# A recommender's interaction network: base tiles by transfers, two contraction tiles to a vector instruction, and one native matmul where three rounded ones stood

## The reference

```python
# e: [2048, 39, 16], field f of sample s is tbl_f[ids[s, f]]
x = e
outs = []
for W in (W0, W1):                       # W0: [128, 39*39], W1: [128, 128*39]
    inter = (x[:, :, None, :] * e[:, None, :, :]).reshape(B, x.shape[1] * 39, 16)
    x = einsum('bid,hi->bhd', inter, W)  # [2048, 128, 16]
    outs.append(x.sum(axis=-1))
h = concatenate(outs + [dense_ctx], axis=1)        # [2048, 272]
h = maximum(h @ W_top1 + b_top1, 0)                # 512
h = maximum(h @ W_top2 + b_top2, 0)                # 256
y = h @ W_top3                                     # [2048, 1]
```

## Time and profile before

| what | value |
|---|---|
| median of 3 runs | 967.51 us (964.41 to 972.47) |
| span of the profiled execution | 1508.4 us |
| PE, DVE, ACT, POOL busy in it | 884.9, 648.8, 600.9, 623.7 us |
| mean granted TensorE clock | 0.788 |
| gathers: number, median, mean, longest | 624, 944 ns, 999 ns, 5595 ns |
| bytes moved by transfers | 88.81 MB |

### The profile page before, as it was taken

One profiled execution on the slowest core, in us unless ns is written; L12 is line 12 of the kernel. 1 busy time (PEld: TensorE's weight loads), 2 busy tenths in 40 slices (PEclk: granted clock), 3 DMA queues, 4 the chain that ended last, 5 costly groups with the idle time before them and its releaser, 6 DMA issues.

```text
span 1508.4 us, 15925 instructions
## 1 busy us (share of the span) xinstructions
PE 884.9 (59%) x3824; PEld 686.1 (45%) x3824; DVE 648.8 (43%) x1012; ACT 600.9 (40%) x1033; POOL 623.7 (41%) x628
## 2 busy tenths in 40 slices
PE   0136393719268292763958367291863936629998
PEld 0014262508146181552846256270642724527886
DVE  2015292617155282442835156160632615427870
ACT  0013282407154171532735154160532714418772
POOL 6756437461714517154271715417054071450000
PEclk9997596759678596785977678595775967859999
DMA  4112142212122132122322122121221312203320
GB/s 130 24 39 61 38 113 52 69 45 66 26 75 61 23 98 68 38 52 51 85 59 58 27 77 71 39 67 25 78 59 18 95 27 70 67 13 101 106 78 3
DMA packets 101439, 88.81 MB, mean 59 GB/s; under 512 B 59925, under 2 KB 71325, under 8 KB 101250
## 3 DMA queue, kind: packets, MB, share of 16 engines
q1 hardware_dynamic: 81410, 83.02, 18.8%
q0 software_dynamic: 19968, 5.15, 3.9%
HBM read 21.35 MB, written 10.49 MB: 21 GB/s over the span
## 4 chain that ended last, share of the span: by engine, by line
PE 38%; another core or an unknown queue 28%; issue 20%; ACT 6%; DVE 4%; POOL 2%; DMA 1%; DVEq 0%; ACTq 0%; SPq 0%; POOLq 0%
PE mlp_ps L440 7%; PE g_ps L429 6%; PE x_ps L400 5%; PE x_ps L397 5%; PE x_ps L398 5%; PE rep_ps L386 3%; POOL e_rows L346 2%; ACT G L589 2%; PE mlp_ps L471 2%; PE mlp_ps L459 2%; DVE products L739 2%; ACT product_hi L572 2%; DVE product_lo L748 1%; PE aux_ps L368 1%
## 5 line engine op out<-in xcount | busy, mean ns | idle before, releaser
L346 POOL DMA_INDIRECT e_rows<-in_tbl_dram,ids_sb x624 | 623.5, 999 | 721.3 <-DMA ids_sb<-in_ids_dram 535.7
L748 DVE TENSOR_TENSOR product_lo<-products,product_hi 117x512 fp32r<-117x512 f32 (+1 forms) x448 | 308.1, 688 | 598.7 <-remote 369.6
L572 ACT CAST product_hi<-products 117x512 fp32r<-117x512 f32 (+1 forms) x448 | 281.4, 628 | 298.7 <-remote 131.2
L400 PE MATMUL x_ps<-product_lo,w_hi 117*128 117x512 f32 (+1 forms) x448 | 199.3, 445 | 176.0 <-issue 91.8
L397 PE MATMUL x_ps<-product_hi,w_hi 117*128 117x512 f32 (+1 forms) x448 | 254.7, 569 | 9.9 <-issue 9.9
L589 ACT COPY G<-g_ps 128x320 f32 (+1 forms) x256 | 189.4, 741 | 38.2 <-remote 24.6
L400 PEld LDWEIGHTS x_ps<-product_lo,w_hi 117*128 117x128 f32 (+1 forms) x448 | 92.5, 207 | 224.1 <-issue 104.5
L398 PE MATMUL x_ps<-product_hi,w_lo 117*128 117x512 f32 (+1 forms) x448 | 190.3, 425 | 0.0
L429 PE MATMUL g_ps<-e_diag,x1T_hi 128*128 128x320 f32 x512 | 134.7, 347 | 92.6 <-issue 58.9
L440 PE MATMUL mlp_ps<-G,w1T 128*128 (+1 forms) x624 | 186.8, 400 | 0.8 <-ACT G L589 0.8
L429 PEld LDWEIGHTS g_ps<-e_diag,x1T_hi 128*128 128x128 f32 x512 | 97.6, 206 | 126.9 <-issue 82.7
(11 more groups left out here) (42 smaller groups left out, 612.7 us busy)
## 6 DMA issues: line engine op xcount, KB each, us to landing
shifted<-cycle SPq DMA_DIRECT2D x128, 234.0 KB
left<-cycle SPq DMA_DIRECT2D x192, 78.0 KB
e_scratch<-e_parts SPq DMA_DIRECT2D x16, 640.0 KB
e_diag<-e_scratch SPq DMA_DIRECT2D x512, 20.0 KB
e_rows<-in_tbl_dram,ids_sb POOLq DMA_INDIRECT x624
shifted<-cycle SPq DMA_DIRECT2D x64, 156.0 KB
w1T<-in_L_rec_W_dram SPq DMA_DIRECT2D x1, 2496.0 KB
G<-in_L_rec_W_dram SPq DMA_DIRECT2D x1, 819.0 KB
```

Of the source, the lines that this page charges most:

```text
L346: nc.gpsimd.indirect_dma_start(out=e_rows[slot][:, f * D:(f + 1) * D], out_offset=None, in_=tables[f], in_offset=bass.IndirectOffsetOnAxis ...
L400: last = nc.tensor.matmul(x1_ps[c % 2][:, :], w0_hi[0:rows, k, :], product_lo[0:rows, (c * KT + k) % LO_RING, :], start=False, stop=(k == ...
L572: nc.scalar.copy(product_hi[0:rows, n % RING, :], products[0:rows, n % RING, :]).then_inc(hi_ready, 1)
L748: nc.vector.tensor_tensor(product_lo[0:rows, n % LO_RING, :], products[0:rows, n % RING, :], product_hi[0:rows, n % RING, :].bitcast(f32), ...
```

## The change

The kernel is written anew around the same arithmetic of the first layer.

- **One tile per batch.** All programs step over 64 chunks `g`, with no loop, and the dense network runs over 128 samples instead of 256: `layer1` has 39 native matmuls of 128 columns for each tile.
- **Base tiles.** The selection matmuls, `rep_ps`, `cycle`, `left` and `shifted` are gone. ACT copies the transposed fields twice over to `eT` (78 partitions, plain float32), and `load_bases` fills five base tiles for each half tile of 1024 columns, with 14 transfers of 39 rows of 4 KB on SP. Each of the seven contraction tiles is a product of two base tiles, both in SBUF.
- **Wide products.** `multiply`, `round_products` and `lower_parts` handle a group of two contraction tiles (1024 elements a partition), and one of one: four instructions of each where there were seven. Products have one buffer.
- **Native G.** `e_diag` and `x1T` stay plain float32, and a quarter of G is one native float32 matmul in place of three float32r ones. The second split (L581's rounding and L759) becomes one plain copy. `e_diag` and its copy in DRAM are half as large.
- **G is copied** with fields outside and the eight samples inside: ACT reads PSUM with a stride and writes runs of eight floats, where it read in order and wrote each float 2 KB from the last.
- **Gathers.** All indices are loaded at the start, and `e_rows` has three slots. `copy_e` on DVE copies a tile twice over to `e_d`, in the first chunk of the tile before it, between `lower_parts` and `multiply`.
- **At the start** ACT issues 32 transfers that assemble the weights.

```diff
+E_SLOTS = 3
...
+STARTS = ((0, 0, 0), (1, 2, 3), (6, 12, 7), (31, 23, 22))
+MIXED = (0, 13)
+BASES = STARTS + (MIXED,)
+PAIRS = ((0, 1), (0, 2), (0, 3), (0, 4), (1, 2), (1, 3), (2, 3))
+NT = len(PAIRS)
+R = 3 * F
+GROUPS = ((0, 1, 2, 0), (0, 3, 2, 2), (1, 2, 2, 4), (2, 3, 1, 6))
+NG = len(GROUPS)
...
+            def load_bases(u):
+                sp.wait_ge(eT_ready, (u // 2 + 1) * ET)
+                after(sp, product_ready, (u - 1) * 2 * NG)
+                half = eT[:, :, :].rearrange("r b d -> r (b d)")[:, u % 2 * HALF:(u % 2 + 1) * HALF]
+                for a, starts in enumerate(BASES):
+                    for n, start in enumerate(starts):
+                        sp.dma_start(bases[u % 2][n * F:(n + 1) * F, a, :],
+                                     half[start:start + F, :]).then_inc(bases_ready[u % 2], 16)
...
+            for t in range(TILES):
+                if t <= 1:
+                    pool.wait_ge(ids_loaded[t], 16)
+                after(pool, e_d_ready, t - E_SLOTS + 1)
+                for f in range(F):
+                    nc.gpsimd.indirect_dma_start(
+                        out=e_rows[t % E_SLOTS][:, f * D:(f + 1) * D], out_offset=None, in_=tables[f],
+                        in_offset=bass.IndirectOffsetOnAxis(ap=ids_sb[:, t, f:f + 1], axis=0),
+                    ).then_inc(gathered[t % E_SLOTS], 16)
...
-                for n, (x, part) in enumerate(((x1T_hi, 0), (x1T_hi, 1), (x1T_lo, 0))):
-                    last = nc.tensor.matmul(g_ps[q % 2][:, :], x[:, q, :], e_diag[c % 2][:, :, q, part, :],
-                                            start=(n == 0), stop=(n == 2))
...
+                nc.tensor.matmul(g_ps[q % 2][:, :], x1T[:, q, :], e_diag[g % 2][:, :, q, :],
+                                 start=True, stop=True).then_inc(e_diag_free if q == Q - 1 else g_in_ps, 1)
...
-                nc.scalar.copy(G[:, :, bass.ds(it % 2 * NB + c * CB + q * QB, QB)].rearrange("i f b -> i b f"),
-                               g_ps[q % 2][:, :].rearrange("i (b f) -> i b f", f=FO)).then_inc(g_ready, 1)
...
+                nc.scalar.copy(G[:, :, t % 2 * TB + c * CB + q * QB:t % 2 * TB + c * CB + (q + 1) * QB],
+                               g_ps[q % 2][:, :].rearrange("i (b f) -> i f b", f=FO)).then_inc(g_ready, 1)
...
+            def copy_e(t):
+                dve.wait_ge(gathered[t % E_SLOTS], (t // E_SLOTS + 1) * 16 * F)
+                after(dve, eT_in_ps, ET * t)
+                after(dve, e_stored, 16 * t)
+                rows = e_rows[t % E_SLOTS][:, :].rearrange("b (n f d) -> b d n f", n=1, d=D)
+                nc.vector.tensor_copy(e_d[:, :, 0:2 * F].rearrange("b d (n f) -> b d n f", f=F),
+                                      rows.to_broadcast([TB, D, 2, F])).then_inc(e_d_ready, 1)
+            def multiply(g, n):
+                a, b, count, first = GROUPS[n]
+                u = g // 2
+                cols = slice(g % 2 * COLS, (g % 2 + 1) * COLS)
+                dve.wait_ge(bases_ready[u % 2], (u // 2 + 1) * 16 * LOADS)
+                after(dve, lo_ready, (g - 1) * NG + n + 1)
+                nc.vector.tensor_tensor(products[:, first:first + count, :], bases[u % 2][:, b:b + count, cols],
+                                        bases[u % 2][:, a:a + 1, cols].to_broadcast([R, count, COLS]),
+                                        ALU.mult).then_inc(product_ready, 1)
+            def lower_parts(g, n):
+                _, _, count, first = GROUPS[n]
+                dve.wait_ge(hi_ready, g * NG + n + 1)
+                after(dve, contracted, (g - 1) * NG + n + 1)
+                nc.vector.tensor_tensor(product_lo[:, first:first + count, :], products[:, first:first + count, :],
+                                        product_hi[:, first:first + count, :].bitcast(f32), ALU.subtract).then_inc(lo_ready, 1)
...
+            copy_e(0)
+            multiply(0, 0)
+            for g in range(CHUNKS):
+                t, c = divmod(g, CPT)
+                multiply(g, 1)
+                lower_parts(g, 0)
+                multiply(g, 2)
+                lower_parts(g, 1)
+                if c == 0 and t + 1 < TILES:
+                    copy_e(t + 1)
+                multiply(g, 3)
+                lower_parts(g, 2)
+                if g + 1 < CHUNKS:
+                    multiply(g + 1, 0)
+                lower_parts(g, 3)
```

More of the change, by code:

```diff
@@ L603, in relu1 @@
-            def relu1(it, pair):
-                act.wait_ge(h1_in_ps, it * 2 + pair + 1)
-                for m in (2 * pair, 2 * pair + 1):
-                    nc.scalar.activation(h1[:, m, :], mlp_ps[:, m % 2, :], ACT.Relu, bias=bias1[:, m:m + 1]).then_inc(h1_ready, 1)
-            def relu2(it):
-                act.wait_ge(h2_in_ps, it + 1)
+                    act.wait_ge(g_in_ps, g * (Q - 1) + q + 1)
+                if c == 0 and q == 0:
+                    after(act, h1_in_ps, M1 * (t - 1))
@@ new lines, in copy_y @@
+            def copy_y(t):
+                act.wait_ge(y_in_ps, t + 1)
+                after(act, y_stored, 16 * t)
+                nc.scalar.copy(y[:, :], mlp_ps[0:1, 2, :]).then_inc(y_ready, 1)
+            act.wait_ge(zeroed, 1)
+            for row, k, j, shift, count in runs:
+                halves = 1 if shift == 0 else 2
+                act.dma_start(w0_both[row:row + count, 0:halves, k, :],
+                              w0[j:j + count, 0:halves, shift, :]).then_inc(w0_loaded, 16)
@@ L654, in _ @@
             for n in range(ET):
-                copy_eT(0, 0, n)
+                copy_eT(0, n)
+            round_products(0, 0)
             act.wait_ge(mlp_loaded, 5 * 16)
-            copy_cycle(0, 0)
-            round_product(0, 0, 0)
-            for c in range(CPI):
-                chunk(0, c, first=True)
-            for c in range(CPI):
-                chunk(1, c, second=True)
-            with act.Fori(2, ITERS - 1) as it:
-                for c in range(CPI):
-                    chunk(it, c)
@@ L697, in _ @@
+            for n in range(2):
+                nc.vector.memset(bases[n][:, len(BASES) - 1, :], 0.0).then_inc(zeroed, 1)
+            for n in range(2):
+                nc.vector.memset(e_diag[n][:, :, :, :], 0.0).then_inc(e_diag_free, 1)
+            nc.vector.memset(e_d[:, :, 2 * F], 1.0)
+            dve.wait_ge(w0_loaded, 16 * len(runs))
+            nc.vector.tensor_tensor(w0_sum, w0_sum, w0_both[:, 1, :, :], ALU.add).then_inc(w0_step, 1)
             dve.wait_ge(w0_step, 1)
-            nc.vector.tensor_tensor(w0_sum, w0_sum, w0_both[:, 1, :, :], ALU.add).then_inc(w0_step, 1)
@@ L786, in _ @@
-            split_hi(0, 0, 0)
-            split_lo(0, 0)
-            multiply(0, 0, 0)
-            for c in range(CPI):
-                chunk(0, c, first=True)
-            with dve.Fori(1, ITERS - 1) as it:
-                for c in range(CPI):
-                    chunk(it, c)
-            end = ITERS - 1
-            for c in range(CPI):
-                chunk(end, c, final=True)
-            lower_x1T(end, CPI - 1)
-            lower_dense(end)
+            dve.wait_ge(dense_loaded, 16 * 3 * GAP // D)
```

739 lines of the change are left out of this document (276 added, 463 removed).

## The result

The changed kernel takes 1069.12 us (median of 4 runs, 1059.68 to 1071.16), the kernel before 969.99 in the same comparison: 1.102 times as long, 95% interval 1.096 to 1.108. The forecast was 1022 us, slower, in a range of 905 to 1090.

What follows compares the result with a forecast made beforehand. The prediction took the kernel before to be bound by gathers that DVE holds, and the changed one more so: 101.8 us of start, 14 tiles at 57.6 and 114 of end make 1022 us, against 967.5; range 905 to 1090.

Steps and rivals of the forecast that it cites:

- The kernel before is bound by its gathers, and something lengthens them: Timed runs of the kernel before: 54.3 us per tile, 5.5 more than bare gathers, against compute of 47.0.
- A gather is held while DVE reads two operands from SBUF: POOL's gathers beside DVE: held during two-SBUF-input instructions, passing when DVE waits or reads one operand from PSUM.
- The rival that rested on it: Gathers beside DVE are not held, so the changed kernel is faster, 895 to 950 us; chance 0.27.
- the rival of a fixed cost: Gathers cost 1.39 us each whatever DVE does, so the time stays the same, 976 us; chance 0.10.
- The residue: A gather meeting a holding DVE instruction waits half of it on average: 0.30 us before, 0.53 after, 1.62 a gather.
- The walk: Other count for a chunk: DVE pairs each ahead of an even 0.84 us wait, two gathers a pair, 1.43 us each.
- The door between adjacent instructions: Assumed that a gather slips in at any boundary of two DVE instructions, which the gather at 217.54 did not.
- the starved rival: Gathers never slip in between adjacent DVE instructions, one passes per wait: 74.5 us a tile, 1259 us; chance 0.10.
- PE's part: Compute on PE falls from 11.75 to 11.4 us a chunk, 45.7 a tile, and isn't the bound.
- the cover of SP's work: SP's queue: 18.9 us of issue in 22.8 for two chunks, hidden by PE's compute at no cost.
- The sum: Whole kernel: 101.8 us to start, 14 tiles of 57.6, 114 at the end, together 1022 us.
- the prediction's view from above: Difference to 967.5 us: gathers' lengthening costs 46, the later place of their waiter 19, the shorter drain gives 14.

Runs made afterwards that it cites:

- before_sb: The kernel before, with the three products a chunk that read `rep_ps` from PSUM reading the cycle tile in SBUF instead; 1012.05 us (1.050).
- the two cadence runs: No computation, only stretches of 39 gathers beside a loop of one kind of instruction, then beside seven DVE widths; 1.252 us a gather beside nothing.
- after_512: The changed kernel with each 1024-wide DVE instruction written as two of 512, also called the 512-wide kernel; 959.89 us (0.994).
- after_13: The changed kernel, but from the fourth tile on with 13 gathers a tile for 39; 953.32 us (0.988).
- the cured kernel: The changed kernel with DVE's products and lower parts both reading their second operand from a constant in PSUM; 957.14 us (0.989).

## Why the prediction was right, and where its sizes were off

*The kernel before is bound by its gathers, and something lengthens them.* Shown: without two thirds of them it takes 896 us. Its compute is 49.5 us a tile, not the 47.0 of the undisturbed stretch, so the gathers add less to compute than I thought, 4.8 us a tile for 7.3.

*A gather is held while DVE reads two operands from SBUF.* Shown from both sides: PSUM operands in after bring back 112 us, the SBUF operand in before costs 46, and by itself the hold gives 2.26 for 1.25 us. The sentence of the Trainium skill (SBUF — State Buffer, Who interferes with whom) on two SBUF inputs agrees with this; its other one, that tensor_tensor was not seen to stall a DMA, does not: here it made the gather, an indirect DMA, take 1.96 us for 0.94. The rival that rested on it, 890 to 950, fell. So did the rival of a fixed cost.

*The residue.* This was the weak step. "Half an instruction, on average" is wrong, because gather and instruction fall into step with each other. The walk's even waits of 0.84 us are not there either: in after DVE runs without a pause from 408.3 to 420.4 us, and then waits 0.98, 2.46 and 2.52 us at a time for `product_hi`. For 1024 columns the rule gave 1.62 us and the walk through a chunk 1.43; I took 1.55 between them, measured are 1.61. With 49.3 us of compute, 1.55 would give 58.3 us a tile, 1.61 gives 59.8: this term is 1.5 us of the 2.2 by which a tile was forecast too short, compute the other 0.7. For 512 columns the same rule was far off (1.45 expected, 1.31 measured, from 110 to 800 us), and for before_sb it missed the other way (22 us forecast, 46 measured). So its agreement with 54.3 us for before was partly luck, and so was how near 1.55 came to 1.61: it was taken between two countings, and neither describes how gathers and waits meet in after.

*The door between adjacent instructions,* on which the starved rival hung: it is there, and in after no gather missed it. But it is not sure. Two gathers of 624 in the two cadence runs were held to the end of the loop, and in before_sb 34 of 220 held gathers missed one or more. The gather at 217.54 was such a one. The starved rival was wrong for after, but what it rested on is real.

*PE's part.* Each record was right. The chain of waits of the 512-wide kernel (start, us, what) has the two of G in 0.54 us for 0.55, and eight of layer1 in 0.89, 0.111 each for 0.115:

```profile
500.15 0.54 PE g_ps L291 x2
...
504.38 0.89 PE z_ps L299 x8
```

Two of the last chunks start 11.07 and 10.87 us after the ones before, for 11.4. Yet a tile takes 51.3 us for 45.7. Named wrong was the cover of SP's work, "PE's 11.4 us a chunk hide it": the mean load on the queue fits, but one `spread` a tile stands behind 14 transfers, and PE then pays the wait of some 3 us and the lower clock after it. The rest of the 5.6 us I can't put down row by row; in after_13 the four chunks of a tile take 10.1, 14.9, 12.1 and 14.1 us. In after this changes little by itself, since gathers bind; it is why the cured kernel stops at 957.

*The sum.* Start 107 for 101.8, fourteen tiles at 59.8 for 57.6, end 124.2 (1067.9 - 943.7) for 114: +5, +31 and +10, 46 of the 47 us by which the forecast was low. At the end 3.2 us lie between the last gather's end (943.7) and the start of the copy (946.9), 91.3 for the forecast 86.8 from there to the last matmul of `x_ps` (1038.2), and 29.7 for 27 behind it. In the prediction's view from above one part is too small: +46, +19 and -14 give 51, not the 54.5 between 967.5 and 1022. From before's split to its drain the rows have 65.0 us (105.8 - 9.3 - 17.1 - 14.4), while 5.8 chunks of 11.75 make 68; the later place of the waiter is worth 22. The sum itself doesn't use that part.

## What to carry to other kernels

Where POOL's gathers bind and DVE's instructions read two operands from SBUF, look at the step of the DVE instructions against the time of one gather: back to back, the cadence is the smallest whole number of steps that fits it, so a width can be nearly twice as bad as a narrower or a wider one, and merging two instructions into one saved DVE 36 us here and cost the kernel 109. Before a DVE instruction is made wider or an operand is moved from PSUM to SBUF, ask who uses the pauses and PSUM reads that go away. And measure it: once the waits are uneven, neither whole steps nor an average gave the number (46 us for 22 or none in before_sb). And the load of a queue says little: ask for the one transfer that stands behind the longest batch, and who waits for it.

## What the runs showed of the hardware that I had not expected

A gather of 0.94 us and DVE fall into step: 1.25 us of cadence beside 512-wide instructions, 2.26 beside 1024-wide, 1.28 beside 1152-wide. A DVE copy of 512 columns with a single SBUF input, 0.335 us a step, holds gathers too (1.484, one of them 9.89 us); in after_512 all 8 gathers that start beside `copy_e` from 110 to 800 us are held, with 1.50 us busy. A gather can miss many ends of instructions: 22.09 us beside 448 columns, until DVE stopped, and 6.31 us in before_sb, eight ends. And after a pause of PE of 2.84 us the granted clock is 0.61 in the mean for 4.4 us, and eight records take 1.55 for 1.06 us.
